# A graph network in 16 pairs of groups: the last state's sum moves from GpSimd to VectorE, a row of attention scores goes through memory, and the order tables change

## The chip, the cores and the metric

One core of one Trainium2 chip runs the whole program. The metric is the device time in microseconds (us) of one execution; before the change it is 1795.21 us, the median of three runs (1795.16 to 1796.53). Engines are called PE (TensorE, matmuls), PEld (its weight loads), DVE (VectorE), ACT (ScalarE), POOL (GpSimd) and SP (SyncE, which issues the DMAs here).

## The reference: what is computed

128 graphs of 128 nodes with 256 features. Layer 0 is three rounds of a gated graph network, layer 1 is graph attention; both have a layer norm and ReLU ahead and a residual behind.

```python
h = relu(layernorm(x)); A = (adj != 0)
for i in range(3):                       # layer 0
    m = einsum('bnd,de->bne', h, weight[i])
    aggr = einsum('bst,bsd->btd', A, m)
    h = gru_cell(aggr, h, w_ih, w_hh, b_ih, b_hh)
x = x + h                                # "the last state added to x"
h = relu(layernorm(x))                   # layer 1
Wh = h @ W.T;  s1 = Wh @ a1;  s2 = Wh @ a2
e = leaky_relu(s1[:, :, None] + s2[:, None, :], 0.2)
e = where(adj == 0, -inf, e);  att = softmax(e)
x = x + einsum('bij,bjo->bio', att, Wh)
```

## The kernel before

Four graphs make a group (512 columns), two groups (a = 0 and 1) make a pair, and there are 16 pairs. The first and the last pair are written out; pairs 1 to 14 are the passes of one hardware loop. Each pair has six slots: slot 0 is group 0 in layer 0, slot 1 is group 1 in layer 0, slots 2 and 3 are layer 1 and slots 4 and 5 layer 2. In a slot PE makes eight gate products, the steps hn, r, in, z for the feature half c = 0 and then for c = 1, of 6, 12, 6 and 12 matmuls (values are split into a high and a low f16 part, so each product takes three matmuls). ACT and DVE turn each product into a gate value, each product has one PSUM bank, and so PE may write a bank again only when ACT or DVE has read it.

All other work stands in the table SIDE: for each engine and each (slot, step) a list of stages that this engine does right after its share of that step. A stage is named by (name, group, ..., pair offset); offset -1 is the pair before, whose attention is done beside the gates of this pair, and +1 is the next pair, whose layer norm is prepared. Each engine works strictly in the order of its own list and waits on semaphores for the others. The order of the tables is thus the whole schedule; PE, ACT, DVE, POOL and SP have a list each. SP's list holds the DMAs; a DMA whose semaphore wait is open holds back all later ones.

The stages that matter here:

- update (DVE, three operations, lines 1144, 1148, 1151): a half of the new state. split_state (ACT line 1038, DVE line 1164) splits it into f16 parts, transpose (SP, line 841) turns them for neighbours (PE lines 433 and 434, ACT line 448 to nb_hi, DVE line 452 to nb_lo). The second half of each r product needs nb_lo.
- split_last, turn_last, add_last, residual: the last state's parts are split, turned by a DMA transpose into h_last, added to each other by POOL (add_last, line 1376, into h_node), and DVE adds h_node to x (residual, line 1180).
- whole_state (POOL, line 1369): adds the two f16 parts of the first state.
- stats_att (DVE, then POOL), apply_att (ACT), split_att, dots (DVE, line 1197): dots makes s1 and s2 of each node, a column of four values each in s12.
- scores: PE turns s2 into a row over all partitions by four transposes of a broadcast column (line 928, bank t_bank); DVE makes the mask (line 1207), adds row and s1 (line 1211), then leaky ReLU, mask, maximum and its negative (lines 1215 to 1223). softmax (ACT line 1055), split_probs, probs_transpose (SP), gather and attend (PE, ACT, DVE) follow.

The head, the tables of the last pair's last slot (LAST_SLOT_SIDE) and the tail (TAIL) have functions of their own.

Of the kernel before, what the change touches and what calls it, by code (L numbers as in the profile page):

```python
# [38 lines left out]
P = 128  # L39
D = 256  # L40
KC = D // P
GROUP = 4
# [27 lines left out]
        (3, 1): [("attend", 0, 0, -1)],  # L70
        (3, 2): [("neighbours", 0, 2, 0, 0)],
        (3, 3): [("attend", 0, 1, -1)],
        (3, 4): [("scores", 1, -1)],
        (3, 6): [("neighbours", 0, 2, 1, 0)],
        (4, 4): [("neighbours", 1, 2, 0, 0)],
        (4, 6): [("neighbours", 1, 2, 1, 0)],
        (4, 7): [("gather", 1, 0, -1)],
        (5, 1): [("neighbours", 0, 0, 0, 1), ("gather", 1, 1, -1)],
        (5, 3): [("attend", 1, 0, -1), ("residual", 0, 0, 0)],
        (5, 4): [("neighbours", 0, 0, 1, 1), ("attend", 1, 1, -1)],  # L80
    },
    "act": {
        (0, 1): [("neighbours", 1, 0, 0, 0), ("split_last", 1, 1, -1), ("apply_att", 0, -1)],
        (0, 2): [("split_att", 0, -1)],
        (0, 5): [("split_state", 0, 1, 0, 0)],
        (0, 6): [("neighbours", 1, 0, 1, 0)],
        (1, 1): [("split_state", 0, 1, 1, 0), ("neighbours", 0, 1, 0, 0)],
        (1, 5): [("scores", 0, -1)],
        (1, 6): [("split_state", 1, 1, 0, 0), ("neighbours", 0, 1, 1, 0)],
        (1, 7): [("softmax", 0, -1)],  # L90
        (2, 0): [("split_state", 1, 1, 1, 0)],
        (2, 2): [("split_probs", 0, -1), ("neighbours", 1, 1, 0, 0), ("apply_att", 1, -1)],
        (2, 3): [("split_att", 1, -1)],
        (2, 4): [("scores", 1, -1)],
        (2, 5): [("neighbours", 1, 1, 1, 0), ("split_state", 0, 2, 0, 0), ("gather", 0, 0, -1)],
        (3, 0): [("gather", 0, 1, -1)],
        (3, 2): [("split_state", 0, 2, 1, 0), ("neighbours", 0, 2, 0, 0)],
        (3, 4): [("split_state", 1, 2, 0, 0)],
        (3, 6): [("neighbours", 0, 2, 1, 0)],
        (3, 7): [("softmax", 1, -1)],  # L100
        (4, 0): [("split_state", 1, 2, 1, 0)],
        (4, 2): [("split_probs", 1, -1)],
        (4, 3): [("neighbours", 1, 2, 0, 0)],
        (4, 4): [("split_last", 0, 0, 0)],
        (4, 5): [("neighbours", 1, 2, 1, 0), ("apply_gnn", 0, 1)],
        (4, 7): [("gather", 1, 0, -1)],
        (5, 0): [("gather", 1, 1, -1), ("split_last", 0, 1, 0)],
        (5, 2): [("neighbours", 0, 0, 0, 1)],
        (5, 3): [("apply_gnn", 1, 1)],
        (5, 4): [("split_last", 1, 0, 0)],  # L110
        (5, 6): [("neighbours", 0, 0, 1, 1)],
# [3 lines left out]
        (0, 1): [("split_last", 1, 1, -1), ("neighbours", 1, 0, 0, 0)],  # L115
        (0, 2): [("dots", 0, 0, -1)],
        (0, 3): [("split_att", 0, -1)],
        (0, 4): [("update", 0, 0, 0, 0)],
        (0, 5): [("residual", 1, 0, -1)],
        (0, 6): [("neighbours", 1, 0, 1, 0)],  # L120
        (0, 7): [("split_state", 0, 1, 0, 0), ("update", 0, 0, 1, 0)],
        (1, 0): [("residual", 1, 1, -1)],
# [11 lines left out]
        (2, 5): [("split_att", 1, -1), ("gather", 0, 0, -1)],
        (2, 6): [("dots", 1, 1, -1)],
        (2, 7): [("update", 0, 1, 1, 0)],
        (3, 1): [("gather", 0, 1, -1)],
        (3, 2): [("split_state", 0, 2, 1, 0)],
        (3, 3): [("neighbours", 0, 2, 0, 0)],
        (3, 4): [("update", 1, 1, 0, 0), ("scores", 1, -1)],  # L140
        (3, 6): [("neighbours", 0, 2, 1, 0), ("split_state", 1, 2, 0, 0), ("adjacency", 0, 1)],
        (3, 7): [("attend", 0, 0, -1)],
        (4, 0): [("update", 1, 1, 1, 0), ("stats_gnn", 0, 1), ("split_state", 1, 2, 1, 0), ("split_probs", 1, -1)],
        (4, 2): [("attend", 0, 1, -1)],
        (4, 3): [("update", 0, 2, 0, 0), ("neighbours", 1, 2, 0, 0), ("split_last", 0, 0, 0)],
        (4, 5): [("neighbours", 1, 2, 1, 0)],
        (4, 6): [("stats_gnn", 1, 1)],
        (4, 7): [("split_gnn", 0, 1), ("gather", 1, 0, -1)],
        (5, 0): [("update", 0, 2, 1, 0), ("split_last", 0, 1, 0)],
        (5, 1): [("gather", 1, 1, -1), ("neighbours", 0, 0, 0, 1)],  # L150
        (5, 2): [("residual", 0, 0, 0), ("update", 1, 2, 0, 0)],
        (5, 3): [("residual", 0, 1, 0)],
# [5 lines left out]
    "pool": {
        (0, 5): [("add_last", 1, 0, -1)],
        (1, 1): [("whole_state", 1, 0, 0)],  # L160
        (1, 5): [("whole_state", 1, 1, 0)],
        (1, 6): [("add_last", 1, 1, -1)],
        (2, 2): [("stats_att", 1, -1)],
        (3, 4): [("stats_gnn", 0, 1)],
        (3, 7): [("stats_gnn", 1, 1)],
        (4, 0): [("add_last", 0, 0, 0)],
        (5, 1): [("add_last", 0, 1, 0), ("stats_att", 0, 0)],
        (5, 2): [("whole_state", 0, 0, 1)],
        (5, 6): [("whole_state", 0, 1, 1)],
    },  # L170
# [91 lines left out]
def graph_blocks(nc, x, adj, weight, w_ih, w_hh, b_ih, b_hh, att_w, att_a, out):  # L262
# [5 lines left out]
    with ctx:  # L268
# [3 lines left out]
        def sem(name):  # L272
            return ctx.enter_context(nc.semaphore(name))
# [1139 lines left out]
```

## Time and profile before

| | |
|---|---|
| median of three runs | 1795.21 us (1795.16 to 1796.53) |
| the profiled execution's own time | 1791.67 us |
| its span, first to last instruction | 1789.9 us |
| PE busy | 1752.7 us, 98% |
| DVE busy | 1547.8 us, 86% |
| ACT busy | 1067.5 us, 60% |
| POOL busy | 436.6 us, 24% |
| mean granted clock of PE | 0.994 |

Busy time is the union of an engine's instructions; matmuls are pipelined, so that the time which one costs in a dense stream is the distance between two starts, not its own duration. A share over the whole span mixes the head (some 35 us), 16 pairs and the tail (the last 35 us); what an engine costs is read from one pair in the steady part.

### The profile page before, as it was taken

The numbers are of one execution on the slowest core, as the hardware profiler recorded it, in microseconds if no ns is written. First come the engines' busy times: TensorE is split into PE (matmuls) and PEld (weight loads), VectorE is DVE, ScalarE is ACT, GpSimd is POOL, SyncE is SP. The second block draws the span as 40 slices with busy tenths as digits, with TensorE's granted clock in tenths as the row PEclk, the third lists the DMA queues.
The fourth block names the chain that finished last, engine by engine and source line by source line (L and its number), as shares of the span: only waits on it lengthen the run. The fifth ranks groups of instructions, "written<-read, shape, count | busy, mean of one in ns | idle before, by whom it ended". The sixth has DMA issues, their size and how long they took to land.

```text
span 1789.9 us, 32218 instructions
## 1 busy us (share of the span) xinstructions
PE 1752.7 (98%) x10260; PEld 918.2 (51%) x10260; DVE 1547.8 (86%) x2887; ACT 1067.5 (60%) x1884; POOL 436.6 (24%) x818
## 2 busy tenths in 40 slices
PE   7999999999999999999999999999999999999995
PEld 5444555545555554555545455554555545555453
DVE  7579898898988889898898988989888898988977
ACT  5466556665556665565665666555666665556543
POOL 2023041321404123041321304124041331414200
PEclk9999999999999999999999999999999999999997
DMA  4225242343424334243343424334243342424321
GB/s 118 65 60 106 53 89 70 81 108 68 94 56 114 70 76 105 45 106 71 73 114 70 94 53 109 79 76 105 41 105 76 70 117 64 83 67 90 68 54 54
DMA packets 387072, 144.10 MB, mean 81 GB/s; under 512 B 302560, under 2 KB 387040, under 8 KB 387040
## 3 DMA queue, kind: packets, MB, share of 16 engines
q1 hardware_dynamic: 387040, 143.71, 35.3%
q8 instruction: 16, 0.26, 0.1%
q14 instruction: 16, 0.13, 0.0%
HBM read 52.96 MB, written 16.78 MB: 39 GB/s over the span
## 4 chain that ended last, share of the span: by engine, by line
PE 83%; DVE 7%; issue 5%; ACT 3%; DVEq 0%; ACTq 0%; POOLq 0%; POOL 0%
PE r_bank L419 24%; PE z_bank L419 23%; PE in_bank L419 13%; PE hn_bank L419 11%; PE s_bank L419 3%; PE w_bank L419 3%; PE nb_bank L434 2%; PE nb_bank L433 2%; ACT relu_att L371 2%; DVE diff L1148 1%; DVE u_lo L1190 1%; PE t_bank L928 1%; DVE diff L1144 1%; DVE n_pre L1130 1%; DVE nb_lo L452 1%
## 5 line engine op out<-in xcount | busy, mean ns | idle before, releaser
L419 PE MATMUL hn_bank<-ht_s,wh_hi 128*128 128x512 f16 x768 | 228.4, 379 | 1.7 <-PEq L534 1.7
L419 PE MATMUL z_bank<-ht_s,wh_hi 128*128 128x512 f16 x768 | 228.4, 379 | 0.0
L419 PE MATMUL r_bank<-ht_s,wh_hi 128*128 128x512 f16 x768 | 228.4, 379 | 0.0
L1021 ACT ACTIVATE n_out<-n_pre,bih 128x512 f32<-128x512 f32 x192 | 137.7, 717 | 150.4 <-DVE n_pre L1135 149.6
L1016 ACT ACTIVATE tanh_r<-r_bank,b_rz,down 128x512 f32<-128x512 f32 x192 | 148.8, 775 | 118.8 <-PE r_bank L419 117.7
L396 POOL TENSOR_TENSOR ln_gnn<-stats_gnn 128x4 f32<-128x4 f32 x32 | 12.1, 380 | 816.6 <-DVE stats_gnn L347 816.6
L448 ACT ACTIVATE nb_hi<-nb_bank 128x512 f16<-128x512 f32 x192 | 113.7, 592 | 150.0 <-PE nb_bank L434 150.0
L1148 DVE SCALAR_TENSOR_TENSOR diff<-tanh_z,diff 128x512 f32<-128x512 f32 x192 | 167.8, 874 | 31.4 <-ACT tanh_z L1025 25.0
L1025 ACT ACTIVATE tanh_z<-z_bank,b_rz,down 128x512 f32<-128x512 f32 x192 | 147.0, 766 | 63.1 <-PE z_bank L419 63.1
L452 DVE TENSOR_TENSOR nb_lo<-nb_bank,nb_hi 128x512 f16<-128x512 f32 x192 | 131.3, 684 | 46.2 <-ACT nb_hi L448 45.7
L1011 ACT ACTIVATE hn_b<-hn_bank,b_hn,down 128x512 f32<-128x512 f32 x192 | 147.7, 769 | 36.1 <-PE hn_bank L419 35.9
L1130 DVE SCALAR_TENSOR_TENSOR n_pre<-tanh_r,hn_b 128x512 f32<-128x512 f32 x192 | 134.2, 699 | 39.5 <-ACT tanh_r L1016 30.8
L1151 DVE SCALAR_TENSOR_TENSOR ht<-diff,n_out 128x512 f32<-128x512 f32 x192 | 162.0, 844 | 6.6
L419 PE MATMUL r_bank<-nb_hi,wi_hi 128*128 128x512 f16 x384 | 145.7, 379 | 7.3 <-DVE nb_lo L452 7.3
L1135 DVE SCALAR_TENSOR_TENSOR n_pre<-in_bank,down,n_pre 128x512 f32<-128x512 f32 x192 | 143.2, 746 | 10.6 <-PE in_bank L419 8.8
L1144 DVE SCALAR_TENSOR_TENSOR diff<-ht,n_out 128x512 f32<-128x512 f32 x192 | 136.1, 709 | 14.0 <-ACT n_out L1021 13.9
L419 PE MATMUL r_bank<-ht_s,wh_lo 128*128 128x512 f16 x384 | 145.5, 379 | 0.0
L419 PE MATMUL r_bank<-nb_lo,wi_hi 128*128 128x512 f16 x384 | 145.5, 379 | 0.0
L419 PE MATMUL r_bank<-nb_hi,wi_lo 128*128 128x512 f16 x384 | 145.5, 379 | 0.0
L419 PE MATMUL in_bank<-nb_hi,wi_hi 128*128 128x512 f16 x384 | 145.5, 379 | 0.0
L419 PE MATMUL in_bank<-nb_lo,wi_hi 128*128 128x512 f16 x384 | 145.5, 379 | 0.0
L419 PE MATMUL in_bank<-nb_hi,wi_lo 128*128 128x512 f16 x384 | 145.5, 379 | 0.0
(252 smaller groups left out, 4008.2 us busy)
## 6 DMA issues: line engine op xcount, KB each, us to landing
x_in<-in_x_dram SPq DMA_DIRECT2D x32, 512.0 KB, 3.8
x_res<-in_x_dram SPq DMA_DIRECT2D x32, 512.0 KB, 4.4
out_dram<-x_out SPq DMA_DIRECT2D x30, 512.0 KB, 5.5
adj_in<-in_adj_dram SPq DMA_DIRECT2D x32, 256.0 KB, 4.0
adj_att<-in_adj_dram SPq DMA_DIRECT2D x32, 256.0 KB, 4.5
h_s<-ht_s SPq DMA_TRANSPOSE x128, 3.0
ht_s<-h_s SPq DMA_TRANSPOSE x64, 3.2
out_dram<-x_out SPq DMA_DIRECT2D x4, 256.0 KB, 2.1
```

Source lines behind the costliest of these rows:

```text
L419: last = nc.tensor.matmul(bank_ap, w, d, start=start and i == 0, stop=stop and i == len(todo) - 1)
L448: nc.scalar.activation(nb_hi[a][:, c, :], nb_bank[:], ACT.Copy).then_inc(nb_hi_ready, 1)
L452: nc.vector.tensor_tensor(nb_lo[a][:, c, :], nb_bank[:], nb_hi[a][:, c, :], ALU.subtract).then_inc(nb_lo_ready, 1)
L1011: nc.scalar.activation(hn_b[c][:], hn_bank[:], ACT.Identity, bias=b_hn[:, c:c + 1], scale=down_gate).then_inc(hn_ready, 1)
L1016: nc.scalar.activation(tanh_r[c][:], r_bank[:], ACT.Tanh, bias=b_rz[:, c:c + 1], scale=down_half).then_inc(tanh_r_ready, 1)
L1021: nc.scalar.activation(n_out[c][:], n_pre[c][:], ACT.Tanh, bias=bih[:, 4 + c:5 + c]).then_inc(n_ready, 1)
L1025: nc.scalar.activation(tanh_z[c][:], z_bank[:], ACT.Tanh, bias=b_rz[:, 2 + c:3 + c], scale=down_half).then_inc(tanh_z_ready, 1)
L1130: nc.vector.scalar_tensor_tensor(n_pre[c][:], tanh_r[c][:], 1.0, hn_b[c][:], ALU.add, ALU.mult).then_inc(rn_ready, 1)
L1135: nc.vector.scalar_tensor_tensor(n_pre[c][:], in_bank[:], down_gate, n_pre[c][:], ALU.mult, ALU.add).then_inc(n_pre_ready, 1)
L1144: nc.vector.scalar_tensor_tensor(diff[c][:], ht[a][:, c, :], 1.0 / HSCALE if layer == 0 else 1.0, n_out[c][:], ALU.mult, ALU.subtract).the ...
L1148: nc.vector.scalar_tensor_tensor(diff[c][:], tanh_z[c][:], 1.0, diff[c][:], ALU.add, ALU.mult).then_inc(zdiff_ready, 1)
L1151: nc.vector.scalar_tensor_tensor(ht[a][:, c, :], diff[c][:], 0.5, n_out[c][:], ALU.mult, ALU.add).then_inc(h_ready, 1)
```

## The change

- add_last and h_node go. DVE's residual now waits for the DMA's landing and adds the two halves of h_last to x itself, in two operations with a semaphore (x_half_ready) between them.
- The row of s2 no longer comes from PE's transposes. s1 and s2 are tensors of their own. SP stores s2 to a buffer in device memory (store_s2) and loads it back broadcast to all partitions (load_s2). ACT adds s1, as its bias, to the row in four operations of 128 columns (scores on ACT); DVE's addition (line 1211) goes, the rest of DVE's scores stays.
- SIDE is laid out anew for all five engines. The work of the other stages, HEAD, LAST_SLOT_SIDE and TAIL are the same (the tail still makes its row on PE).

```diff
 "pe":
-        (0, 2): [("neighbours", 1, 0, 0, 0), ...],
+        (0, 4): [("neighbours", 1, 0, 0, 0)],
         (0, 5): [("neighbours", 1, 0, 1, 0)],
-        (2, 7): [("gather", 0, 0, -1)],
-        (3, 0): [("gather", 0, 1, -1)],
+        (3, 2): [("scores", 0, -1), ("gather", 0, 0, -1), ("neighbours", 0, 2, 0, 0)],
+        (3, 4): [("gather", 0, 1, -1)],
 "act":
-        (0, 1): [("neighbours", 1, 0, 0, 0), ("split_last", 1, 1, -1), ("apply_att", 0, -1)],
+        (0, 1): [("split_last", 1, 1, -1), ("apply_att", 0, -1)],
+        (0, 2): [("neighbours", 1, 0, 0, 0)],
+        (1, 6): [("split_state", 1, 1, 0, 0), ("scores", 0, -1)],
+        (2, 3): [("softmax", 0, -1), ("split_probs", 0, -1)],
+        (3, 6): [("scores", 1, -1)],
 "dve":
-        (0, 6): [("neighbours", 1, 0, 1, 0)],
-        (1, 2): [("split_state", 0, 1, 1, 0), ("dots", 0, 1, -1)],
-        (1, 7): [("scores", 0, -1), ("update", 1, 0, 1, 0)],
+        (0, 3): [("neighbours", 1, 0, 0, 0), ("update", 0, 0, 0, 0), ("split_att", 0, -1)],
+        (0, 4): [("split_state", 0, 1, 0, 0)],
+        (0, 5): [("neighbours", 1, 0, 1, 0)],
+        (0, 6): [("residual", 1, 0, -1), ("update", 0, 0, 1, 0)],
+        (0, 7): [("dots", 0, 1, -1)],
+        (1, 0): [("split_state", 0, 1, 1, 0)],
+        (1, 1): [("residual", 1, 1, -1)],
+        (1, 2): [("neighbours", 0, 1, 0, 0)],
+        (1, 3): [("stats_att", 1, -1)],
+        (1, 4): [("update", 1, 0, 0, 0)],
+        (1, 5): [("neighbours", 0, 1, 1, 0)],
+        (1, 7): [("split_state", 1, 1, 0, 0)],
+        (2, 0): [("scores", 0, -1), ("update", 1, 0, 1, 0)],
+        (2, 2): [("neighbours", 1, 1, 0, 0), ("split_state", 1, 1, 1, 0), ("dots", 1, 0, -1), ("update", 0, 1, 0, 0)],
+        (2, 3): [("split_probs", 0, -1), ("split_state", 0, 2, 0, 0)],
+        (2, 6): [("neighbours", 1, 1, 1, 0), ("update", 0, 1, 1, 0), ("split_att", 1, -1)],
+        (2, 7): [("dots", 1, 1, -1), ("split_state", 0, 2, 1, 0)],
+        (3, 0): [("gather", 0, 0, -1), ("stats_gnn", 0, 1)],
 "pool":
-        (0, 5): [("add_last", 1, 0, -1)],
+        (0, 1): [("whole_state", 1, 0, 0)],
+        (0, 5): [("stats_att", 1, -1)],
+        (1, 3): [("whole_state", 1, 1, 0)],
 "sp":
+        (0, 0): [("turn_last", 1, 1, -1), ("transpose", 0, 1, 0, 0)],
+        (0, 3): [("store_s2", 0, -1)],
+        (0, 7): [("transpose", 0, 1, 1, 0)],
+        (1, 0): [("load_s2", 0, -1)],
+        (1, 2): [("transpose", 1, 1, 0, 0)],
+        (3, 0): [("store_s2", 1, -1)],
+        (3, 1): [("transpose", 0, 2, 1, 0)],
+        (3, 3): [("load_s2", 1, -1)],
 ...
+                def store_s2(p, a):
+                    sp.wait_ge(dots_ready, per_group(p, a))
+                    sp.dma_start(s2_dram[a], s2[a][:]).then_inc(s2_stored[a], 16)
+
+                def load_s2(p, a):
+                    sp.wait_ge(s2_stored[a], per_load(p))
+                    wait_reached(sp, sum_ready, per_group(p, a) - 1)
+                    sp.dma_start(s2_row[:].rearrange("q t b -> q (t b)"),
+                                 s2_dram[a].rearrange("t b -> (t b)").unsqueeze(0).broadcast_to(
+                                     [P, T])).then_inc(s2_landed[a], 16)
 ...
-                def scores(p, a):
-                    pe.wait_ge(dots_ready, per_group(p, a))
-                    ...
-                    for b in range(GROUP):
-                        last = nc.tensor.transpose(t_bank[:, b * P:(b + 1) * P],
-                                                   s12[a][:, b, 1:2].broadcast_to([P, P]), ident[:])
 ...
+                def scores(p, a):
+                    act.wait_ge(s2_landed[a], per_load(p))
+                    wait_reached(act, minus_max_ready, per_group(p, a) - 1)
+                    for b in range(GROUP):
+                        last = nc.scalar.activation(score[:, b, :], s2_row[:, :, b], ACT.Identity,
+                                                    bias=s1[a][:, b:b + 1])
+                    last.then_inc(sum_ready, 1)
 ...
                     if not after_gates(p):
-                        dve.wait_ge(h_node_ready, per_chunk(p, a, c))
-                        nc.vector.scalar_tensor_tensor(part, h_node[c][:], 1.0 / HSCALE, part, ALU.mult,
+                        dve.wait_ge(h_last_landed[a][c], per_load(p))
+                        nc.vector.scalar_tensor_tensor(part, h_last[:, c, 0], 1.0 / HSCALE, part, ALU.mult,
+                                                       ALU.add).then_inc(x_half_ready, 1)
+                        dve.wait_ge(x_half_ready, per_chunk(p, a, c))
+                        nc.vector.scalar_tensor_tensor(part, h_last[:, c, 1], 1.0 / HSCALE, part, ALU.mult,
                                                        ALU.add).then_inc(x1_ready, 1)
 ...
-                    dve.wait_ge(s2_done, n)
-                    wait_reached(dve, prob_ready, n - 1)
-                    nc.vector.tensor_tensor(score[:], t_bank[:].rearrange("p (b t) -> p b t", b=GROUP),
-                                            s12[a][:, :, 0:1].broadcast_to([P, GROUP, P]),
-                                            ALU.add).then_inc(sum_ready, 1)
```

## Rows read from the trace of the kernel before

**Rows 1.** The page: the span, and busy time of each engine.

```profile
span 1789.9 us, 32218 instructions
PE 1752.7 (98%) x10260; PEld 918.2 (51%) x10260; DVE 1547.8 (86%) x2887; ACT 1067.5 (60%) x1884; POOL 436.6 (24%) x818
```

**Rows 2.** Busy time by engine over whole pairs: the first loop pass and the last.

```profile
core 0: us, PE busy (x) PEld busy (x) DVE busy (x) ACT busy (x) POOL busy (x), PEclk, DMA share, GB/s
133.60:242.90 109.30, 107.58 (x633) 55.82 (x632) 97.26 (x180) 65.72 (x117) 29.50 (x56) 1.00 0.39 78
...
1538.40:1646.30 107.90, 107.58 (x633) 55.86 (x632) 95.50 (x177) 65.81 (x117) 28.53 (x53) 1.00 0.37 83
```

**Rows 3.** What PE waited for, its repeated wait: total us, times, longest.

```profile
PE r_bank L419 <- DVE nb_lo L452: 7.3, 15, 1.7
```

**Rows 4.** PE in order of time around one scores stage: start, duration, instruction.

```profile
165.14 0.38 PE L419 MATMUL in_bank<-nb_hi,wi_lo 128*128 128x512 f16 x1
165.36 0.60 PE L928 MATMUL t_bank<-ident,s 128*128 128x128 f32 x4
165.80 0.22 PE L433 MATMUL nb_bank<-adj_s,h_s 128*128 128x128 f16 x1
```

**Rows 5.** PE, then DVE, in order of time in slot 1 of one pair.

```profile
910.40 0.39 PE L419 MATMUL r_bank<-nb_hi,wi_hi 128*128 128x512 f16 x1 [0.37 <-DVE nb_lo L452]
...
909.00 0.74 DVE L1135 SCALAR_TENSOR_TENSOR n_pre<-in_bank,down,n_pre 128x512 f32<-128x512 f32 x1
909.66 0.68 DVE L452 TENSOR_TENSOR nb_lo<-nb_bank,nb_hi 128x512 f16<-128x512 f32 x1
```

**Rows 6.** DVE, then POOL, in order of time in slot 0 of the same pair.

```profile
900.84 1.37 DVE L1197 CUSTOM_DVE_ANT_0 dot_terms<-relu_att,c 128x256 f32<-128x256 f32 x1
...
903.43 0.41 DVE L1197 CUSTOM_DVE_ANT_0 dot_terms<-relu_att,c 128x256 f32<-128x256 f32 x1
...
899.47 1.16 POOL L1376 TENSOR_TENSOR h_node<-h_last 128x512 f32<-128x512 f16 x1 [3.23 <-DMA h_last<-ht_s]
900.58 2.63 POOL L1369 TENSOR_TENSOR ht<-ht_s 128x512 f32<-128x512 f16 x2
```

**Rows 7.** Groups by line and form: count, busy us, mean ns, idle before.

```profile
L1148 DVE SCALAR_TENSOR_TENSOR diff<-tanh_z,diff 128x512 f32<-128x512 f32 x192 | 167.8, 874 | 31.4 <-ACT tanh_z L1025 25.0
L1197 DVE CUSTOM_DVE_ANT_0 dot_terms<-relu_att,c 128x256 f32<-128x256 f32 x240 | 123.1, 568 | 0.1
L1376 POOL TENSOR_TENSOR h_node<-h_last 128x512 f32<-128x512 f16 x60 | 78.6, 1310 | 163.7 <-DMA h_last<-ht_s 163.7
L1180 DVE SCALAR_TENSOR_TENSOR x_res<-h_node,x_res 128x512 f32<-128x512 f32 x60 | 41.0, 683 | 0.0
L1055 ACT ACTIVATE prob<-score,minus_max 128x128 f32<-128x128 f32 x120 | 46.5, 390 | 19.7 <-DVE minus_max L1223 19.7
L1211 DVE TENSOR_TENSOR score<-t_bank,s 128x512 f32<-128x512 f32 x30 | 20.6, 688 | 6.1 <-PE t_bank L928 6.1
```

**Rows 8.** Single lines: duration in ns, lowest, median, highest.

```profile
L1148 DVE SCALAR_TENSOR_TENSOR diff<-tanh_z,diff x192: 691/693/1690, 44.8 to 1756.5; 128x512 f32<-128x512 f32 x192
...
L1197 DVE CUSTOM_DVE_ANT_0 dot_terms<-relu_att,c x240: 413/421/1369, 143.8 to 1700.5; 128x256 f32<-128x256 f32 x120
```

**Rows 9.** DMA issues: count, KB each, median us from issue to landing.

```profile
out_dram<-x_out SPq DMA_DIRECT2D x30, 512.0 KB, 5.5
...
out_dram<-x_out SPq DMA_DIRECT2D x4, 256.0 KB, 2.1
...
att_col<-in_L_gnn_a_dram SPq DMA_DIRECT2D x1, 2.0 KB, 7.5
```

**Rows 10.** One pair's first half in stretches of 18 us, columns as in rows 2.

```profile
890.76:908.74 17.98, 17.98 (x97) 8.63 (x95) 17.40 (x26) 10.54 (x17) 10.30 (x8) 1.00 0.56 131
908.74:926.70 17.96, 17.59 (x96) 8.60 (x95) 17.68 (x36) 9.88 (x15) 4.78 (x11) 1.00 0.46 109
926.70:944.70 18.00, 18.00 (x115) 9.38 (x114) 14.48 (x35) 12.54 (x27) 0.00 (x0) 1.00 0.30 66
```

More of the change, by code:

```diff
@@ L70 @@
[L70 to L80, printed above, removed]
+        (1, 0): [("residual", 0, 1, -1)],
@@ L94 @@
[L94 to L103, printed above, removed]
@@ L104 @@
-        (4, 4): [("split_last", 0, 0, 0)],
[L105 to L109, printed above, removed]
+        (0, 1): [("split_last", 1, 1, -1), ("apply_att", 0, -1)],
+        (0, 2): [("neighbours", 1, 0, 0, 0)],
+        (0, 3): [("split_att", 0, -1)],
+        (0, 4): [("neighbours", 1, 0, 1, 0), ("split_state", 0, 1, 0, 0)],
@@ L114 @@
         (0, 0): [("update", 1, 2, 1, -1)],
-        (0, 1): [("split_last", 1, 1, -1), ("neighbours", 1, 0, 0, 0)],
+        (0, 1): [("split_last", 1, 1, -1)],
         (0, 2): [("dots", 0, 0, -1)],
[L117 to L122, printed above, removed]
-        (1, 2): [("split_state", 0, 1, 1, 0), ("dots", 0, 1, -1)],
@@ L134 @@
[L134 to L138, printed above, removed]
-        (3, 3): [("neighbours", 0, 2, 0, 0)],
[L140 to L152, printed above, removed]
@@ new lines @@
+        (4, 1): [("attend", 0, 0, -1), ("attend", 0, 1, -1)],
+        (4, 2): [("split_state", 1, 2, 1, 0)],
+        (4, 3): [("split_probs", 1, -1)],
+        (4, 4): [("neighbours", 1, 2, 0, 0), ("update", 0, 2, 0, 0), ("split_last", 0, 0, 0)],
+        (4, 6): [("split_gnn", 0, 1), ("neighbours", 1, 2, 1, 0)],
+        (4, 7): [("gather", 1, 0, -1)],
+        (5, 0): [("update", 0, 2, 1, 0), ("adjacency", 1, 1), ("split_last", 0, 1, 0)],
+        (5, 1): [("stats_gnn", 1, 1), ("neighbours", 0, 0, 0, 1)],
@@ L157 @@
+        (5, 2): [("gather", 1, 1, -1), ("attend", 1, 0, -1), ("residual", 0, 0, 0)],
+        (5, 3): [("update", 1, 2, 0, 0)],
+        (5, 4): [("residual", 0, 1, 0), ("split_last", 1, 0, 0), ("stats_att", 0, 0), ("attend", 1, 1, -1)],
+        (5, 5): [("neighbours", 0, 0, 1, 1)],
+        (5, 7): [("split_gnn", 1, 1)],
     },
     "pool": {
[L159 to L162 removed]
@@ L709, in graph_blocks @@
         u_lo = both("u_lo", [P, GROUP, D], F16)
-        s12 = both("s12", [P, GROUP, 2], F32)
+        s1 = both("s1", [P, GROUP], F32)
+        s2 = both("s2", [P, GROUP], F32)
+        s2_row = sb("s2_row", [P, P, GROUP], F32)
+        s2_dram = [nc.dram_tensor(f"s2_dram{a}", [P, GROUP], F32, kind="Internal").ap() for a in range(2)]
         row_scale = both("row_scale", [P, GROUP], F32)
```

147 lines of the change are left out of this document (68 added, 79 removed).

## The prediction

> **What bounds the kernel now.** I read the page first. PE is busy 98% of the span and DVE 86% [rows 1]. A dense PE can still be waiting inside, so the second view is a whole pair: in the last loop pass PE is busy 107.58 of 107.90 us at a clock share of 1.00 [rows 2]. Adding up PE's work says the same. Two starts of 512-column matmuls lie 0.216 us apart (0.22 in the rows, [rows 4]) and a pair has 12 x 36 = 432 of them, 93.3 us. Twelve neighbours stages of 0.44 us (165.80 to 166.24, where the next product starts) are 5.3, four half gathers 2.7, four half attends 5.2 and two scores 0.9. Together that is 107.4 us. PE's stream is the bound, and any work on another engine costs time only where PE waits for it.
>
> Third, PE's waits: one repeats in the steady part, the second half of an r product waiting for nb_lo, 7.3 us over 15 times, 1.7 of it in one case [rows 3]. Its other waits have one or two cases each, in the head and the tail, whose code stays. The reader should see why that wait exists [rows 5]: the PE row idles 0.37 us until DVE's nb_lo, 909.66 plus 0.68, is written. DVE was not waiting for anything: it is busy 17.40 and 17.68 us of the first two 18 us stretches of the pair [rows 10]. It is simply late. The third stretch is looser, 14.48.
>
> **Why DVE is late there.** Rows 6 show the cause. A dot takes 0.41 us, but 1.37 while POOL runs its 128x512 sums. The same shows over the run: line 1148 has median 693 ns, highest 1690 and mean 874, line 1197 median 421, highest 1369 and mean 568 [rows 7, 8]. So each POOL sum holds up one DVE instruction, by up to 0.96 us. POOL makes 60 sums for the last state [rows 7] and 64 for the first state. The Trainium skill ("SBUF — State Buffer", SBUF: two separate sides) says that the pair of ports which both engines share is locked for a whole instruction, against DVE instructions with two SBUF inputs; by that rule the new additions can be held up by the sums that stay. The trace agrees as far as it goes, with 1.37 against 0.41 us.
>
> **The change, part by part.**
>
> PE loses the scores transposes. Four of them push the next stage from 165.36 to 165.80 [rows 4], 0.44 us. There are 30 stages (two groups, pairs 0 to 14; DVE's addition that reads them stands in 30 records [rows 7]), so 30 x 0.44 = 13.2 us. All of it lies on the path, as PE's stream is the bound. Note that neither the 0.60 of the row nor the sum of busy time is the price, since matmuls overlap.
>
> POOL loses 60 sums, 78.6 us [rows 7]. POOL's own time bounds nothing. What is bought is DVE time: at most 0.96 us each [rows 6], 57 us; at least (192 x 0.181 + 240 x 0.147) / 124 = 0.57 us each from the two lines above alone, 34 us. Other lines are stretched too, so I take 0.8, 48 us, or 3.2 us in a pair.
>
> DVE gains 60 additions of about 0.683 us, 41.0 us, and loses 30 of 0.688, 20.6 us [rows 7]. The second addition has an f16 input and waits for the first, which no row shows; between 0.6 (the distance of two independent starts, [rows 5]) and 0.8 us nothing changes below. In a pair: 95.5 - 3.2 + 2.8 - 1.4 = 93.7 us, for 106.7 us of PE. DVE gets looser, not tighter, and costs nothing by its sum.
>
> ACT gains 120 activations of 128 columns. The nearest row is the exponential of the same size with the same kind of bias, 0.390 us [rows 7]: 3.1 us in a pair on top of 65.7 [rows 2]. The new read takes every fourth element, for which no row exists; twice the row, 0.78, gives 6.2 us. Even so ACT is at 72 of 107. It costs nothing, as long as its row has landed.
>
> SP gains two DMAs for each group: a store of 2 KB and a load of one 2 KB row into 128 partitions, 256 KB. Bounds from rows: a 256 KB store in the quiet tail lands after 2.1 us, a 512 KB one after 5.5, and a tiny load in the crowded head after 7.5 [rows 9]. So the round trip takes 4.2 to 13.0 us; the load is most like the tail's store, and I take 6. Here the Trainium skill speaks against the change: "DMA: Bandwidth & Descriptors" (Anatomy of one DMA) gives every DMA a fixed cost of about 2.0 us, most of it the receipt from memory, plus bytes at 436 GB/s. An estimate by that page is 4.6 us in place of 0.44 us on PE. It would change the sum only if the row were on the path.
>
> Is it? dots for group 0 are finished by the last entry of slot 0. DVE's own work in slot 0, to the end of dots, is three updates (6.5 us), four gate operations (2.7), split_last, split_state and two neighbours (2.6), two halves of dots (2.8), split_att (1.2) and two additions (1.3), 17.1 us, and with its waits for ACT and two held-up instructions 20 to 22 us after the slot's start. ACT comes to its scores after step (1, 6), that is after one slot (15.6 + 0.9 us) and 12 us of the next, at 28 to 31. So the row has about 9 us, against the 6 that I expect. For group 1 (dots at (2, 7), ACT at (3, 6)) the distance is about the same. A late row stops ACT, and behind it stand the two gate activations of z and the next hn; PE reaches the banks that these free about 3 us later, so PE feels the round trip only from about 12 us.
>
> What SP's new waits hold up: store_s2 waits for dots, and transpose(0,1,1,0) stands behind it, but its own input is written by DVE after dots anyway; likewise transpose(0,2,1,0) for group 1. load_s2 waits some 2 to 5 us for its store, while transpose(1,1,0,0) behind it needs a half that DVE splits 8 us later. No hold-up of PE comes out.
>
> **The new order.** It decides whether the 7.3 us go too and whether another wait appears. DVE's work in slots 0 and 1 in the old table, with 0.65 us for an independent 512-column operation (0.66 between the two starts in [rows 5]), is five updates (10.8), gates 5.4, four neighbours 2.6, dots 2.8, scores 3.5, the rest 6.5, and six held-up instructions 5: about 37 us for 35 us of PE. That is the backlog of rows 10. In the new table one update and the scores leave slots 0 and 1, the residuals add 1.3 and three hold-ups go: about 30 us. Moreover nb_lo of group 1 stands at (0, 5), ahead of in, residual and update, while before it stood behind them. So the old wait should go, 7.3 us.
>
> What is late next is slot 2. Until nb_lo at (2, 6), DVE must do scores 2.8, two updates 4.3, four gate operations 2.7, three neighbours and split stages and that nb_lo itself 2.6, half of dots 1.4, split_probs 1.1, and perhaps one hold-up 0.8: 15.7 us. It starts about 1.6 us after PE enters the slot, so it ends at 17.3. PE needs it after slot 2 (15.6 + 0.9) and 2.6 us of slot 3, at 19.1. The slack is 1.8 us. This is the tightest place that I find; slot 3 has only about 10 us of DVE work for 19 us of PE and clears the rest. Two slots have PE's neighbours later than before, which loosens them.
>
> **The sum.** 1791.67 (the profiled execution) - 13.2 - 7.3 = 1771.2 us. The median of the runs stands 3.5 us above that execution, so 1774.7, rounded to 1775.
>
> **Rivals.** (a) A wait of PE stays. The transposes go, but DVE or ACT is still late in one place of each pair, most likely in slot 2 where 1.8 us is all there is. For it speaks that the old table had such a wait; against it, that DVE's load in slots 0 and 1 falls by 7 us. With the old size the time is 1782; with 1 us in each of 15 pairs it is 1790. This is also the case in which the new layout doesn't do what it seems to. (b) The slower side: the row's round trip. Each us beyond 12 stops PE 30 times. It eats up all of the gain at 12.7 us, is over 0.2% slower (3.6 us) from 12.8, and at the upper bound of 13.0 gives 1775 + 30 = 1805. For it speaks only the 7.5 us of the head, taken with several large loads in the queue; in the loop it has short transposes ahead of it. (c) What DVE is relieved of comes back: if the sums that stay hold up two instructions each, DVE has no more than before, which is case (a) with a smaller wait.
>
> **Chances.** No repeated wait, 1772 to 1778: 0.58. A wait of 0.2 to 1 us in each pair, 1778 to 1790: 0.30, all of it still faster by over 0.2%. The late row, 1792 and more: 0.06, most of it slower. Something that I have not found, spread over both sides: 0.06. The likeliest case gives the number. The range is 1771 to 1789: it takes in most of (a), and below the forecast only the first loop pass (109.30 against 107.90 us) and the 0.2 us a pair that my sum of PE's work leaves open. With 0.2% (3.6 us) as about what a measurement of this kernel can tell from no change: faster 0.88, the same 0.04, slower 0.08.
>
> **What would show it.** A middle pair takes 106.7 us in the profile after. The r product's wait for nb_lo is gone from PE's waits. Line 1148's and the dots' means fall, and DVE is busy about 93.7 us in a pair. ACT's wait for the landed row is absent or short, and no PE wait names ACT. I am wrong if a PE wait with a count of 15 or 30 has taken the old one's place, if ACT idles for a DMA before its scores, or if the pair is shorter by 0.9 us only.

## The result, and the profile after

The changed kernel takes 1769.49 us (median of four runs, 1769.14 to 1769.67) against 1795.62 us for the kernel before, measured beside it (1795.16 to 1796.53). The ratio is 0.9854, with a 95% interval of 0.9837 to 0.9871. The gain is 26.1 us. I had forecast 1775 with a range of 1771 to 1789: the direction and most of the steps held, the number lies 1.5 us below the range.

The head of the page:

```profile
span 1767.9 us, 32098 instructions
PE 1736.1 (98%) x10140; PEld 905.0 (51%) x10140; DVE 1496.5 (85%) x2917; ACT 1104.4 (62%) x2004; POOL 309.9 (18%) x758
```

Busy time over a first, a middle and a last loop pass, with columns as in rows 2:

```profile
134.57:241.09 106.52, 106.52 (x625) 55.00 (x624) 92.65 (x179) 68.38 (x125) 20.61 (x52) 1.00 0.40 85
880.21:986.73 106.52, 106.52 (x625) 55.00 (x624) 92.38 (x179) 68.34 (x125) 20.17 (x49) 1.00 0.38 89
1519.34:1625.86 106.52, 106.52 (x625) 55.01 (x624) 92.52 (x179) 68.37 (x125) 20.11 (x50) 1.00 0.39 89
```

PE is busy to the last digit of these rows, 106.52 of 106.52 us, and the three passes are alike. In rows 2 the first pass was 1.4 us longer than the last, and PE idled in both. What PE still waits for, longest first, is the head and the tail:

```profile
PE hn_bank L962 <- DVE s L1296: 8.7, 2, 8.0
PE setup_bank L573 <- DMA raw_ih<-in_L_gnn_w_ih_dram: 6.4, 2, 5.5
```

The wait for nb_lo [rows 3] is not in this view any more. The new row of scores, as SP's issues, then ACT, in slots 0 and 1 of one pair:

```profile
901.92 0.34 SPq L854 DMA_DIRECT2D s_dram<-s  x1
902.86 1.24 SPq L838 DMA_TRANSPOSE h_s<-ht_s  x1
905.25 0.34 SPq L859 DMA_DIRECT2D s_row<-s_dram  x1
...
912.38 1.77 ACT L1051 ACTIVATE score<-s_row,s 128x128 f32<-128x128 f32 x4
```

and the two DMAs by median landing:

```profile
s_row<-s_dram SPq DMA_DIRECT2D x30, 256.0 KB, 3.4
...
s_dram<-s SPq DMA_DIRECT2D x30, 2.0 KB, 2.4
```

The store goes out at 901.92, and ACT takes the row at 912.38 without having waited (the row has no bracket). That is 10.5 us for a round trip of about 6 (2.4 + 3.4 and the issue).

### The profile page after: what moved, and what is told of

Same layout as the page of the kernel before. It is cut to its first block, busy times and chain, and to the rows that moved or that the text cites. A ratio compares the mean times of both kernels' runs of the same rounds, so it can differ in the third digit from the quotient of the medians.

```text
span 1767.9 us, 32098 instructions
## 1 busy us (share of the span) xinstructions
PE 1736.1 (98%) x10140; PEld 905.0 (51%) x10140; DVE 1496.5 (85%) x2917; ACT 1104.4 (62%) x2004; POOL 309.9 (18%) x758
## 4 chain that ended last, share of the span: by engine, by line
PE 96%; DVE 1%; issue 1%; POOLq 0%; POOL 0%; ACT 0%; DVEq 0%
PE r_bank L412 28%; PE z_bank L412 28%; PE hn_bank L412 14%; PE in_bank L412 14%; PE s_bank L412 4%; PE w_bank L412 3%; PE nb_bank L427 2%; PE nb_bank L426 2%; DVE u_lo L1342 0%; DVE dot_terms L1296 0%; DVE x_out L1252 0%; DVE tail_max L1327 0%; DVE vt_lo L1241 0%; DVE stats_att L340 0%; POOLq L814 0%
## 5 line engine op out<-in xcount | busy, mean ns | idle before, releaser
L1133 DVE SCALAR_TENSOR_TENSOR n_pre<-tanh_r,hn_b 128x512 f32<-128x512 f32 x192 | 145.5, 758 | 82.1 <-ACT tanh_r L1011 78.8
L1370 POOL TENSOR_TENSOR ht<-ht_s 128x512 f32<-128x512 f16 x64 | 86.4, 1350 | 470.2 <-DMA ht_s<-h_s 352.2
L1151 DVE SCALAR_TENSOR_TENSOR diff<-tanh_z,diff 128x512 f32<-128x512 f32 x192 | 138.4, 721 | 9.4 <-ACT tanh_z L1020 2.2
L412 PE MATMUL z_bank<-ht_s,wh_lo 128*128 128x512 f16 x384 | 145.5, 379 | 0.0
L412 PE MATMUL z_bank<-nb_hi,wi_hi 128*128 128x512 f16 x384 | 145.5, 379 | 0.0
```

Source lines behind the costliest of these rows:

```text
L412: last = nc.tensor.matmul(bank_ap, w, d, start=start and i == 0, stop=stop and i == len(todo) - 1)
L1133: nc.vector.scalar_tensor_tensor(n_pre[c][:], tanh_r[c][:], 1.0, hn_b[c][:], ALU.add, ALU.mult).then_inc(rn_ready, 1)
L1151: nc.vector.scalar_tensor_tensor(diff[c][:], tanh_z[c][:], 1.0, diff[c][:], ALU.add, ALU.mult).then_inc(zdiff_ready, 1)
L1370: nc.gpsimd.tensor_tensor(ht[a][:, c, :], ht_s[0][a][:, c, 0, :], ht_s[0][a][:, c, 1, :], ALU.add).then_inc(ht_ready, 1)
```

## The experiments

Two theories stand against each other. **Stream:** the time is PE's stream; each part of the change is worth what it takes out of the stream, the transposes or a wait. **DVE load:** DVE had too much work, and POOL's sums or the new layout are what the gain needs. Beside them stands the question where the 5 us of gain beyond the forecast came from.

**The kernel before, once more.** No edit. My profiled execution and the timed runs stood 3.5 us apart.

> The kernel before, unchanged, profiled once more. The profiled execution of before took 1791.67 us while its timed runs took 1795.2 to 1796.5. Theory A (the one repeated PE wait, the r product for nb_lo in slot 1, differs from execution to execution): the new profile shows a span that differs from 1789.9 by about 1.1 times the change of that wait's total (7.3 us before). Theory B (a constant cost outside the span): the span is again 1789.9 +- 0.5 with the wait at 7.3, and the time above it differs. Ratio 1.000 either way.

Measured: 1795.9 us, ratio 1.0002 (0.9992 to 1.0012); the profiled span is 1793.4, not 1789.9. PE's wait (total us, times, longest):

```profile
PE r_bank L419 <- DVE nb_lo L452: 10.0, 15, 1.6
```

and busy time over two of its passes:

```profile
1000.53:1108.71 108.18, 107.57 (x634) 55.86 (x633) 95.88 (x177) 65.83 (x117) 26.94 (x53) 1.00 0.35 82
1108.71:1216.61 107.90, 107.56 (x634) 55.85 (x633) 95.48 (x177) 65.84 (x117) 28.23 (x53) 1.00 0.36 83
```

Theory A holds in the main: the wait is 10.0 us here and 7.3 in [rows 3], which is 2.7 of the 3.5 us between the two spans. Of the rest, 0.2 us lies in the head and some 0.5 us behind the start of the last pair. The wait also comes in a longer and a shorter form. PE in order of time, in the pass of 108.18 us and in the one of 107.90:

```profile
1019.32 0.38 PE L419 MATMUL r_bank<-ht_s,wh_lo 128*128 128x512 f16 x1
1020.31 0.39 PE L419 MATMUL r_bank<-nb_hi,wi_hi 128*128 128x512 f16 x1 [0.61 <-DVE nb_lo L452]
...
1127.50 0.38 PE L419 MATMUL r_bank<-ht_s,wh_lo 128*128 128x512 f16 x1
1128.21 0.39 PE L419 MATMUL r_bank<-nb_hi,wi_hi 128*128 128x512 f16 x1 [0.34 <-DVE nb_lo L452]
```

What differs stands at the head of the pair. In order of time DVE in the long pass and in the short one, then POOL in the long pass and in the short one:

```profile
1001.29 2.24 DVE L364 SCALAR_TENSOR_TENSOR h_s<-relu_gnn,h_s 128x512 f16<-128x512 f32 x2
...
1109.47 1.28 DVE L364 SCALAR_TENSOR_TENSOR h_s<-relu_gnn,h_s 128x512 f16<-128x512 f32 x2
...
1000.95 0.48 POOL L413 TENSOR_TENSOR ln_att<-ln_att 128x4 f32<-128x4 f32 x1
1001.38 3.16 POOL L1369 TENSOR_TENSOR ht<-ht_s 128x512 f32<-128x512 f16 x2
...
1109.13 2.29 POOL L413 TENSOR_TENSOR ln_att<-ln_att 128x4 f32<-128x4 f32 x1
1111.37 2.71 POOL L1369 TENSOR_TENSOR ht<-ht_s 128x512 f32<-128x512 f16 x2
```

In both passes POOL's small instruction starts 0.42 us after the pair's start, beside the same instructions of DVE. In the short pass it takes 2.29 us, and POOL's large sums start 2.7 us after the pair's start; in the long one it takes 0.48, the sums start after 0.85 us, and DVE's h_s beside them takes 2.24 in place of 1.28 us. Of pairs 2 to 15 the first execution has one with a held-up h_s, this one twelve. In all 28 the two go together: the bracket is at least 0.60 us where h_s was held up and at most 0.53 where it was not. That the one causes the other is not shown by an experiment, nor why POOL or DVE comes first in a given pass.

Note also the price of a wait. The bracket says 0.34 and 0.61 us, but the two starts lie 0.71 and 0.99 us apart where 0.216 is the pace: 0.49 and 0.77 us lost.

**Only the order of two entries.**

```diff
 "act":
-        (0, 5): [("split_state", 0, 1, 0, 0)],
-        (0, 6): [("neighbours", 1, 0, 1, 0)],
+        (0, 5): [("neighbours", 1, 0, 1, 0), ("split_state", 0, 1, 0, 0)],
 "dve":
-        (0, 5): [("residual", 1, 0, -1)],
-        (0, 6): [("neighbours", 1, 0, 1, 0)],
+        (0, 5): [("neighbours", 1, 0, 1, 0), ("residual", 1, 0, -1)],
```

> The kernel before with two entries moved: neighbours of group 1, half 1, stands one step earlier on ACT (ahead of split_state) and on DVE (ahead of residual and the in operation). Nothing of the work changes. Theory (order alone removes the wait): PE's wait for nb_lo in slot 1 is gone; counted by the distance of the two matmul starts (0.75 - 0.22 = 0.53 us each, 9.8 us in all) the profiled span falls from 1789.9 to about 1780, and the timed runs to 1782 to 1786. Rival (DVE has too much work in slots 0 and 1, so the wait only moves): the span stays above 1787 and another wait with a count near 15 appears.

Measured: 1784.16 us, ratio 0.9936 (0.9919 to 0.9952). A middle pass:

```profile
887.30:994.70 107.40, 107.40 (x634) 55.94 (x633) 95.94 (x177) 65.36 (x117) 27.70 (x53) 1.00 0.36 83
```

PE is full again, with DVE at 95.9 us, all of POOL's sums in place and all the transposes. One wait of 0.37 us is left, in the first loop pass. So an order of two entries is worth 11.4 us, and the wait goes without any of DVE's load being taken away.

**DVE adds both halves, old order.**

```diff
 "pool":
-        (0, 5): [("add_last", 1, 0, -1)],
 ...
-                        dve.wait_ge(h_node_ready, per_chunk(p, a, c))
-                        nc.vector.scalar_tensor_tensor(part, h_node[c][:], 1.0 / HSCALE, part, ALU.mult,
+                        dve.wait_ge(h_last_landed[a][c], per_load(p))
+                        nc.vector.scalar_tensor_tensor(part, h_last[:, c, 0], 1.0 / HSCALE, part, ALU.mult,
+                                                       ALU.add).then_inc(h_node_ready, 1)
+                        dve.wait_ge(h_node_ready, per_chunk(p, a, c))
+                        nc.vector.scalar_tensor_tensor(part, h_last[:, c, 1], 1.0 / HSCALE, part, ALU.mult,
 ...
```

> The kernel before with one part of the change alone: POOL's sum of the last state's halves is gone and DVE adds both halves to x, in the old order tables. Theory (POOL's sums cost DVE more than the second addition): DVE's busy time falls by 60 x (0.85 - 0.68) or about 10 us, the slot 1 wait shrinks or goes, and the time is 1784 to 1793. Rival (DVE's queue in slots 0 and 1 gets longer by the second addition): the wait grows, and the time is 1796 to 1805.

Measured: 1783.37 us, ratio 0.9932 (0.9916 to 0.9949), just below the low end that I gave, with no wait of PE in any of the 15 pairs:

```profile
886.20:993.60 107.40, 107.40 (x633) 55.93 (x632) 94.86 (x181) 65.72 (x117) 21.30 (x49) 1.00 0.36 83
```

DVE's busy time is 1536.1 us, 11.7 less than in rows 1 (15.0 less than in the second profile of the kernel before). A POOL sum thus cost DVE 0.2 us more than the second addition that replaces it. This edit removes the same wait that the order alone removes: the two are substitutes, not terms of one sum.

**The transposes alone, put back into the changed kernel.** PE makes them at their old places, (1, 6) and (3, 4), and nobody reads them; DVE's dots wait until the transposes before have read s2.

```diff
+                def scores(p, a):
+                    pe.wait_ge(dots_ready, per_group(p, a))
+                    for b in range(GROUP):
+                        last = nc.tensor.transpose(t_bank[:, b * P:(b + 1) * P],
+                                                   s2[a][:, b:b + 1].broadcast_to([P, P]), ident[:])
+                    last.then_inc(s2_done, 1)
 ...
```

> The changed kernel with PE's four score transposes put back for each group, at their old places, and their result used by nobody. It prices the transposes alone. Theory (PE's stream is the bound, 0.44 us a stage): 30 x 0.44 = 13.2 us more, 1782.7 us, a middle pair of 107.40 us. Rival (a part of their price was hidden, or they cost the 0.60 us of their row): below 1778, or 1787.5.

Measured: 1783.31 us, 13.8 more than the changed kernel (ratio to before 0.993, 0.9914 to 0.9947); the span is 1781.7, again 13.8 more. A middle pass:

```profile
886.53:993.92 107.39, 107.39 (x633) 55.95 (x632) 91.88 (x179) 68.36 (x125) 19.97 (x49) 1.00 0.39 88
```

It is 0.87 us longer for two stages, so 0.435 us each, 13.05 us for 30. Of the 0.7 us that remain, the head accounts for 0.2 (PE enters pair 0 at 36.2 instead of 36.0 us) and the last pair with the tail for 0.5, of unknown cause.

**The row through memory and ACT's sum alone, old order.** POOL's sums stay.

```diff
 "act":
-        (1, 5): [("scores", 0, -1)],
-        (1, 6): [("split_state", 1, 1, 0, 0), ("neighbours", 0, 1, 1, 0)],
-        (2, 4): [("scores", 1, -1)],
+        (1, 6): [("split_state", 1, 1, 0, 0), ("neighbours", 0, 1, 1, 0), ("scores", 0, -1)],
+        (3, 3): [("scores", 1, -1)],
 "sp":
-        (1, 4): [("transpose", 0, 1, 1, 0)],
+        (1, 4): [("transpose", 0, 1, 1, 0), ("store_s2", 0, -1), ("load_s2", 0, -1)],
-        (2, 5): [("transpose", 0, 2, 0, 0), ("transpose", 0, 2, 1, 0)],
+        (2, 5): [("transpose", 0, 2, 0, 0), ("store_s2", 1, -1), ("load_s2", 1, -1), ("transpose", 0, 2, 1, 0)],
 ...
```

> The other part of the change alone in the old tables: s2's row through memory and the score sum on ACT; POOL's sums and DVE's single addition stay. The store and load stand right behind transpose(0,1,1,0) and transpose(0,2,0,0) on SP, ACT's scores at (1,6) and (3,3). Theory (the parts add: the transposes are 0.435 us a stage, the slot 1 wait comes before all of this and stays): 1795.6 - 13.1 = 1782.5 us, a middle pair 107.0 to 107.4 us with the wait for nb_lo still at 15. Rival (the row comes too late in this order): ACT waits for the landing and PE for ACT; 1790 or more.

Measured: 1782.26 us, ratio 0.9926 (0.991 to 0.9943), within 0.3 us of the expected number. ACT waits for the row, 23.1 us over 15 times, without harm. From the second loop pass on a pass takes 106.9 to 107.5 us, as the wait for nb_lo stays. PE's wait (total us, times, longest) is where it was:

```profile
PE r_bank L417 <- DVE nb_lo L450: 9.7, 15, 1.6
```

**Both parts, old order.** The two edits above together; only the layout of the tables is left out.

> Both parts of the change in the old tables (with the same places for the row as in row_old_order); only the new layout is left out. Theory (the sum on DVE alone already removed the slot 1 wait, 1783.4 us, and the transposes are another 13.1): 1770.3 us, a middle pair of 106.52 us, the same as the changed kernel within 0.1%; the layout then buys nothing in time. Rival (the layout is needed to hold both): a wait appears in slot 1 or 2, 1773 to 1785.

Measured: 1769.91 us, ratio 0.9859 (0.9843 to 0.9875), against 0.9854 (0.9837 to 0.9871) for the changed kernel. A middle pass takes 106.5 us. Two passes of this execution are longer (107.19 and 106.76 us); in the one profile of the changed kernel all 14 take 106.52. So the new layout gave no time that these runs can tell from nothing.

**The sum back on POOL, new order.**

```diff
 "pool":
-        (0, 1): [("whole_state", 1, 0, 0)],
+        (0, 1): [("whole_state", 1, 0, 0), ("add_last", 1, 0, -1)],
+        (0, 4): [("add_last", 1, 1, -1)],
-        (4, 4): [("stats_gnn", 0, 1)],
+        (4, 4): [("stats_gnn", 0, 1), ("add_last", 0, 0, 0)],
-        (5, 2): [("stats_gnn", 1, 1)],
+        (5, 2): [("stats_gnn", 1, 1), ("add_last", 0, 1, 0)],
 ...
```

> The changed kernel with the sum of the last state's halves back on POOL (four 128x512 sums a pair) and one addition on DVE, in the new tables. Theory (DVE has room in the new order, so what POOL's sums hold up is covered): 1769 to 1771 us, DVE's busy time up by 60 x (0.85 - 0.68) = 10 us, no PE wait. Rival (POOL's hold-ups are what made PE wait): a wait with a count near 15 comes back, 1774 to 1783.

Measured: 1770.26 us, ratio 0.9861 (0.9844 to 0.9877). Busy time on the page:

```profile
PE 1737.6 (98%) x10140; PEld 905.9 (51%) x10140; DVE 1518.9 (86%) x2857; ACT 1103.4 (62%) x2004; POOL 406.8 (23%) x818
```

DVE's busy time is 22.4 us more than in the changed kernel, twice what I expected, and no steady wait returned. In the new order DVE's relief is worth 0.8 us at most, which these runs can't tell from nothing.

**A late row.**

```diff
 "sp":
-        (1, 0): [("load_s2", 0, -1)],
-        (1, 2): [("transpose", 1, 1, 0, 0)],
+        (1, 2): [("transpose", 1, 1, 0, 0), ("load_s2", 0, -1)],
```

> The changed kernel with group 0's load of the row moved on SP behind transpose(1,1,0,0), so that it lands some 38 us after the pair's start where ACT would begin its sum at 32.2. It prices a late row. Theory (ACT stands still, and PE reaches what stands behind it with 1.1 to 2.3 us to spare): ACT waits 5.5 to 6 us in each pair for the landing, PE loses 3.5 to 5 us of each of 15 pairs, 1822 to 1845 us. Rival (my figure before the result, PE feels it only 3 us later and later slots give back): 1800 to 1818 us. If the row were hidden anyway: below 1773.

Measured: 1870.71 us, ratio 1.0422 (1.0404 to 1.0439): 101 us more than the changed kernel, above every figure that I gave. ACT's wait for the row is 115.0 us in 15 (7.7 each, not 5.5 to 6), since the load left at 965.83, 36.5 us after the pair's start. PE's wait (total us, times, longest):

```profile
PE z_bank L411 <- ACT tanh_z L1019: 71.9, 15, 6.0
```

PE in order of time around it, in one pair:

```profile
967.18 0.38 PE L411 MATMUL in_bank<-nb_hi,wi_lo 128*128 128x512 f16 x1
972.03 1.04 PE L411 MATMUL z_bank<-ht_s,wh_hi 128*128 128x512 f16 x2 [4.47 <-ACT tanh_z L1019]
972.86 0.63 PE L411 MATMUL z_bank<-ht_s,wh_lo 128*128 128x512 f16 x1
...
975.23 0.38 PE L411 MATMUL z_bank<-nb_hi,wi_lo 128*128 128x512 f16 x1
...
976.10 0.22 PE L425 MATMUL nb_bank<-adj_s,h_s 128*128 128x128 f16 x1
```

Busy time and, third from the end, the granted clock just behind the wait:

```profile
972.00:975.00 3.00, 2.97 (x8) 1.05 (x9) 2.86 (x6) 3.00 (x6) 0.00 (x0) 0.50 0.00 0
975.00:980.00 5.00, 5.00 (x31) 2.51 (x30) 4.29 (x14) 4.47 (x11) 0.00 (x0) 1.00 0.01 1
```

PE loses 4.6 us between the starts 967.18 and 972.03 (less the pace of 0.216), and then the 12 matmuls of z take 4.07 us (972.03 to 976.10) instead of 2.59, because the clock is granted at 0.50, 1.2 in place of 2.4 GHz, for 3 us. That is 4.6 + 1.5 = 6.1 us, and this pass, of 112.6 us, is 6.1 longer than 106.52. The slow clock makes such a wait a third dearer than its own length. The 15 pairs lose more than 15 x 6.1 = 92 us, because the first ones wait longer (up to 6.0 us) and because in five pairs the clock is low for twice as long, as here in the first loop pass:

```profile
176.31:183.13 6.82, 4.39 (x11) 1.60 (x12) 5.33 (x9) 6.62 (x12) 0.00 (x0) 0.50 0.00 0
```

Loop passes with such a stretch take 113.5 to 115.3 us.

**More work for DVE at the tightest place.** Three, then five instructions of 128x512 behind the scores at (2, 0):

```diff
-        (2, 0): [("scores", 0, -1), ("update", 1, 0, 1, 0)],
+        (2, 0): [("scores", 0, -1), ("extra", 0, -1), ("update", 1, 0, 1, 0)],
 ...
+                def extra(p, a):
+                    for k in range(3):
+                        nc.vector.scalar_tensor_tensor(extra_out[:, k], c12[:], 1.0, c12[:], ALU.mult, ALU.add)
```

> The changed kernel with three DVE instructions more in each pair (128x512, from a constant tile to a scratch tile that nobody reads), right behind the scores of group 0 at (2,0). It tests the slack of the tightest place. My figure before the result was 1.8 us until nb_lo at (2,6): three instructions of 0.65 us are 1.95, so 0.15 us late, 1769 to 1772 us. The trace of the changed kernel shows two idle stretches of DVE before it (0.85 and 0.48 us) and 1.07 us behind it, 2.4 us in all: no change, 1769.5 us, and no PE wait. Rival (DVE has no room there): 29 us more.

Measured: 1769.83 us, ratio 0.9859 (0.9843 to 0.9875): no change from the changed kernel, and no wait of PE for nb_lo.

> The same with five instructions more, 3.25 us. By my 1.8 us of slack: 1.45 us late in each of 15 pairs, 1791 us. By the 2.4 us of the trace: 0.85 us late, 1782 us, with a PE wait for nb_lo of a count near 15 in slot 3. If it is absorbed: below 1773.

Measured: 1776.07 us, ratio 0.9892 (0.9876 to 0.9909), 6.6 us more than the changed kernel. PE's wait (total us, times, longest):

```profile
PE r_bank L412 <- DVE nb_lo L445: 3.2, 15, 0.2
```

and busy time over a middle pass:

```profile
882.70:989.60 106.90, 106.69 (x625) 54.93 (x624) 95.13 (x184) 68.81 (x125) 20.01 (x49) 1.00 0.38 88
```

The wait stands where I had placed it, 0.39 us by the length of the passes (106.91 against 106.52). DVE in order of time, the five and what follows them:

```profile
920.15 3.09 DVE L1229 SCALAR_TENSOR_TENSOR extra_out<-c 128x512 f32<-128x512 f32 x5
923.15 0.69 DVE L1148 SCALAR_TENSOR_TENSOR diff<-ht,n_out 128x512 f32<-128x512 f32 x1
```

By the distance of starts the five take 3.0 us, 0.60 each and not 0.65. So the slack was 3.0 - 0.39 = 2.6 us: more than my 1.8, and close to the 2.4 that I had read from the trace of after.

**The row laid out graph by graph.**

```diff
-        s2_row = sb("s2_row", [P, P, GROUP], F32)
-        s2_dram = [nc.dram_tensor(f"s2_dram{a}", [P, GROUP], F32, kind="Internal").ap() for a in range(2)]
+        s2_row = sb("s2_row", [P, GROUP, P], F32)
+        s2_dram = [nc.dram_tensor(f"s2_dram{a}", [GROUP, P], F32, kind="Internal").ap() for a in range(2)]
 ...
-                        last = nc.scalar.activation(score[:, b, :], s2_row[:, :, b], ACT.Identity,
+                        last = nc.scalar.activation(score[:, b, :], s2_row[:, b, :], ACT.Identity,
```

> The changed kernel with the row laid out graph by graph, so that ACT's four sums read 128 neighbouring columns and not every fourth; the store then scatters values of four bytes. ACT's sum took 0.521 us with the step of 16 bytes, the exponential of the same size 0.390. Theory (the step costs ACT 0.13 us an instruction): 0.39 us now, the store's landing gets longer, and the time stays at 1769.5 +- 1. Rival (the bias and the Identity function cost it): 0.52 us again.

Measured: 1815.85 us (1811.03 to 1819.17), ratio 1.0114 (1.0091 to 1.0137). The sum on ACT in the changed kernel (lowest, median, highest ns):

```profile
L1051 ACT ACTIVATE score<-s_row,s x120: 504/521/535, 166.7 to 1692.8; 128x128 f32<-128x128 f32 x120
```

the same line here:

```profile
L1052 ACT ACTIVATE score<-s_row,s x120: 384/387/403, 169.5 to 1735.5; 128x128 f32<-128x128 f32 x120
```

the store's median landing here:

```profile
s_dram<-s SPq DMA_DIRECT2D x30, 2.0 KB, 7.6
```

and the waits here, PE's costliest and that of SP's queue for the store (total us, times, longest):

```profile
PE nb_bank L426 <- DMA h_s<-ht_s: 32.8, 19, 3.1
...
SPq L860 <- DMA s_dram<-s: 182.8, 30, 8.9
```

The step in the read does cost ACT 0.13 us an instruction, as expected. But the store of scattered 4-byte values lands after 7.6 us in place of 2.4. ACT waits for the row (29.5 us over 23 times), but no repeated wait of PE names ACT. The load's wait for its store stands in SP's queue, 182.8 us in place of 11.5 in the changed kernel, and the state transposes behind it reach PE late. I expected no change in time and got 46 us more, so "the time stays" was wrong; it is a late store that costs here, through the queue and not through ACT.

## Why the prediction was wrong, step by step

**The bound held.** PE's stream gives the time, before and after: 107.40 us a pair with transposes, 106.52 without, whatever DVE, ACT and POOL do beside it, as long as PE has no wait (four kernels at 106.5, three at 107.4).

**The transposes were right:** 13.2 us forecast, 13.05 by the length of the passes. To read the price from the distance of starts, not from the row's 0.60 or from the busy time, was what made it right.

**The wait was mis-sized, and that is the step that failed.** The sum takes 7.3 us for the wait for nb_lo, from [rows 3], and carries the 3.5 us between the profiled execution and the median over as if they would stay. Measured on the medians, the wait was worth about 13 us: with 1795.6 as the start, 13.0 us for the transposes leave 13.1, and the order of two entries (11.4 us) and the sum on DVE (12.2 us) each measure nearly all of it without touching the transposes. The two parts of the error are these.

First, a bracket as in [rows 5] counts idle time only from the modelled end of the matmul ahead, 0.38 us after its start, while the pace is 0.216. Each wait costs 0.16 us more than its bracket (0.49 for 0.34 above), 2.4 us over 15. I had used the distance of starts for the transposes and not for the wait. In the profiled spans the account then closes: 1789.9 - 13.05 - 7.3 - 2.4 + 1.0 (the head, where PE enters pair 0 at 36.0 instead of 35.0 us) = 1768.2, against 1767.9 measured. The 1.0 us is no price of the change: in the 13 profiled executions, all with the same head, that start lies anywhere from 35.0 to 36.4 us.

Second, the 3.5 us were not a constant. The profiled execution that I started from was a short one: the second profile of the kernel before has a span of 1793.4 us and a wait of 10.0 us, so 2.7 of the 3.5 us between the two are that wait, mostly in its longer form. That the timed executions had it in this form too is likely and not shown, as they have no trace. The changed kernel has no such wait, and its profiled execution, 1769.67 us, lies 0.2 us from its median. The forecast was 5.2 us too high: 3.5 of it from this and 2.4 from the bracket, less 1.0 for the head; 0.3 are left. The range had the same fault: below the forecast it left room for the first pass and for PE's work, and for no larger wait.

**DVE's account was right in sign and too small.** I forecast 93.7 us a pair and the rows show 92.4 to 92.7; a POOL sum costs DVE about 0.9 us in the old order (0.68 for the addition and 0.2) and 1.1 in the new (22.4 us over 60 and 0.68), not 0.8. As forecast, the mean of line 1148's operation (diff<-tanh_z) fell, from 874 to 721 ns, and that of the dots from 568 to 418. The additions take 681 and 692 ns, as expected. But what I argued from it, that the lighter load in slots 0 and 1 and the new order together remove the wait, can't be kept in that form: an earlier place of nb_lo is enough, and so is a lighter load, and in the old order the whole gain is there (1769.91 us). I gave the layout a part that the runs don't show. Nor does the order of the update tell the tables apart, as I wrote: one update stands ahead of that nb_lo and one behind it in both, at (0, 4) and (0, 7) before and (0, 3) and (0, 6) after. What moved ahead of it is the in operation and residual.

**The row through memory was right.** 6 us forecast for the round trip, 2.4 + 3.4 and the issue measured; 9 us of room forecast, 10.5 measured. The estimate of 4.6 us by the Trainium skill ("DMA: Bandwidth & Descriptors", Anatomy of one DMA) came out low. That section gives its 2.0 us for DMAs that GpSimd issues, not for every DMA as I wrote, and these are SP's. The point from which lateness costs was too generous, though: I let PE feel it 3 us after ACT, and with the late row 7.7 us of ACT's wait became 4.6 us of PE's, some 3 us later as said, but with 1.5 us of slow clock on top, which the sum lacked. The late row was a real danger with a steeper price than I gave it.

**The tightest place was right:** nb_lo at (2, 6) is where DVE's extra work first reaches PE. Its slack was 2.6 us, not 1.8; my 0.65 us for each independent operation, where the starts lie 0.60 apart, is part of the difference.

**ACT's price** was 0.521 us for each sum, between my 0.390 and 0.78, and nothing hung on it.

## What to carry to other kernels

When one engine's stream is full, price each removed thing by the distance of two starts in that stream, waits as well as instructions; an idle figure that starts at a modelled end is too small. A gap between one profiled execution and the median of the runs may hold the very wait that the change removes, so profile the kernel before twice ahead of carrying it over as a constant. When a change removes a wait by several means at once, try each alone: here an exchange of two entries, or one sum moved, was enough, and neither they nor the new layout add up.

## What the runs showed of the hardware that I had not expected

ACT reads 128 f32 values with a step of 16 bytes in 521 ns and neighbouring ones in 387 ns. The Trainium skill ("SBUF — State Buffer", Specifications) says that the memory has lines of 16 bytes and that an access wants at least two hits in a line; the two rows agree in direction.

A DMA of 2 KB lands after 2.4 us as 128 pieces of 16 bytes and after 7.6 us as 512 pieces of 4 bytes; the bytes are the same, so it is the pieces that cost; whether by their number or by their size these two cases can't tell.

DVE's and POOL's instructions are both stretched where they run side by side: POOL's 128x4 instruction took 2.29 or 0.48 us beside the same instructions of DVE, and DVE's took up to 1.69 us. Which of the two was stretched at the head of a pair went with the pair's length in the kernel before, about 107.9 or 108.2 us.

At the end of a wait of some 4.5 us PE's granted clock fell to 0.50, its level of 1.2 GHz, and stood there for 3 us; in passes with waits of 0.3 to 0.6 us, and in the first loop pass with its 1.7 us, the rows show 1.00 throughout. With the row laid out graph by graph, the clock fell to 0.50 behind four of the five longest waits between the head and the tail (2.5 to 3.1 us), below behind the one that ended at 1693.4 us, and behind none of the shorter ones:

```profile
1694.50:1697.90 3.40, 3.40 (x9) 1.21 (x8) 2.50 (x5) 3.00 (x8) 0.00 (x0) 0.50 0.09 26
```
